# A two-layer transformer step on one NeuronCore: the terms of the last attention row are split two and two between GpSimd and VectorE, and every engine of the second layer gets another order

## The reference

```python
xn = _layernorm(x)
x = x + _L0_attn_ref(xn, ...) + _L0_ffn_ref(xn, ...)       # causal softmax attention, 16 heads of 64; gated FFN, 384 hidden
xn = _layernorm(x)
x = x + _L1_attn_ref(xn, ...) + _L1_ffn_ref(xn, ...)
```

```python
def step(W, qkvb_t):
    q_t, k_t, v_t, b_t = qkvb_t
    v_old = jnp.einsum('bhij,bhj->bhi', W, k_t)
    delta = b_t * (v_t - v_old)
    W_new = W + delta[..., :, None] * k_t[..., None, :]
    out_t = jnp.einsum('bhij,bhj->bhi', W_new, q_t)
    return (W_new, out_t)
```

## Time and profile before

| | before |
|---|---|
| median of 3 runs | 1667.04 us (1667.03 to 1667.09) |
| the profiled execution, its own time | 1666.79 us |
| its span, from the first to the last instruction | 1665.1 us |
| granted TensorE clock | 1.000 |
| busy: PE, weight load, DVE, ACT, POOL | 99%, 63%, 80%, 60%, 53% |
| instructions: PE, DVE, ACT, POOL | 9922, 2760, 2014, 685 |
| second layer, from VectorE's first step of it on | 1150.3 us to the end |

### The profile page before, as it was taken

One profiled execution on the slowest core, in us unless ns is written; L12 is line 12 of the kernel. 1 busy time (PEld: TensorE's weight loads), 2 busy tenths in 40 slices (PEclk: granted clock), 3 DMA queues, 4 the chain that ended last, 5 costly groups with the idle time before them and its releaser, 6 DMA issues.

```text
span 1665.1 us, 29161 instructions
## 1 busy us (share of the span) xinstructions
PE 1651.0 (99%) x9922; PEld 1043.5 (63%) x9922; DVE 1326.7 (80%) x2760; ACT 1002.1 (60%) x2014; POOL 885.7 (53%) x685
## 2 busy tenths in 40 slices
PE   9999999999999999999999999999999999999998
PEld 6566656665665566556655665555667767776767
DVE  5477777777777777777777777776999999999997
ACT  3256656665666566666666666666676666566562
POOL 2133333333433333433333433343999999999995
PEclk9999999999999999999999999999999999999999
DMA  8000000000000000000000000010000000000000
GB/s 181 26 1 1 1 1 1 2 1 1 1 1 1 1 1 1 1 1 1 2 1 1 1 1 1 2 26 1 1 1 7 7 1 7 1 7 7 1 7 14
DMA packets 30036, 13.55 MB, mean 8 GB/s; under 512 B 17066, under 2 KB 29380, under 8 KB 29892
## 3 DMA queue, kind: packets, MB, share of 16 engines
q1 hardware_dynamic: 29892, 11.70, 3.1%
HBM read 9.60 MB, written 2.10 MB: 7 GB/s over the span
## 4 chain that ended last, share of the span: by engine, by line
PE 95%; DVE 2%; issue 1%; ACT 1%; POOL 1%; SPq 0%; DMA 0%; DVEq 0%; ACTq 0%; POOLq 0%
PE pair L946 17%; PE flip L963 16%; PE accum L984 11%; PE pair L2692 9%; PE misc L911 7%; PE flip L2715 5%; PE misc L1030 4%; PE flip L2704 4%; PE misc L924 3%; PE accum L1008 3%; PE flip L2752 3%; PE accum L2704 2%; PE pair L874 2%; PE accum L2715 2%; PE accum L1012 2%; PE flip L2738 1%
## 5 line engine op out<-in xcount | busy, mean ns | idle before, releaser
L382 POOL TENSOR_SCALAR probs<-probs,recip 128x256 f32<-128x256 f32 (+5 forms) x448 | 331.3, 754 | 693.8 <-DVE recip L616 693.8
L457 ACT ACTIVATE probs<-pair,neg_max 128x768 f32<-128x768 f32 (+5 forms) x448 | 332.3, 750 | 209.2 <-DVE neg_max L598 209.2
L598 DVE TENSOR_REDUCE neg_max<-pair 128x1 f32<-128x768 f32 (+7 forms) x512 | 372.8, 754 | 32.6 <-PE pair L946 9.6
L963 PEld LDWEIGHTS flip<-ident,probs 128*128 128x128 f32 x2048 | 228.0, 141 | 142.3 <-issue 65.4
L946 PE MATMUL pair<-qk_sb 64*128 64x512 f32 (+3 forms) x1536 | 292.1, 505 | 1.8 <-ACT probs L457 1.0
L963 PE MATMUL flip<-ident,probs 128*128 128x128 f32 x2048 | 280.1, 277 | 1.8 <-ACT slots L419 1.8
L419 ACT ACTIVATE slots<-flip 128x512 f32<-128x512 f32 x320 | 183.8, 595 | 155.6 <-PE flip L963 155.6
L589 DVE TENSOR_TENSOR pair<-pair,mask 128x128 f32<-128x128 f32 x512 | 137.1, 292 | 80.2 <-PE pair L946 80.2
L984 PE MATMUL accum<-slots,v_sb 128*64 128x512 f32 (+3 forms) x1024 | 192.7, 519 | 0.0
L2692 PE MATMUL pair<-slow_sb,h_T 128*128 128x512 f32 x384 | 179.9, 594 | 1.2 <-ACT probs_last L457 1.0
L1524 POOL TENSOR_TENSOR prod<-xnT,qs 128x1024 f32<-128x1024 f32 (+3 forms) x32 | 180.2, 5639 | 0.9 <-DVE qs L2233 0.9
(11 more groups left out here) (216 smaller groups left out, 2538.7 us busy)
## 6 DMA issues: line engine op xcount, KB each, us to landing
out<-x SPq DMA_DIRECT2D x8, 256.0 KB, 2.3
x<-in_L_attn_x SPq DMA_DIRECT2D x3, 512.0 KB, 5.6
slow_sb<-in_L_attn_w_slow SPq DMA_DIRECT2D x3, 512.0 KB, 8.2
w_qk<-in_L_attn_qkv_w SPq DMA_DIRECT2D x2, 512.0 KB, 7.2
xn<-in_L_ffn_W SPq DMA_DIRECT2D x1, 1024.0 KB
x<-in_L_attn_x SPq DMA_DIRECT2D x2, 256.0 KB, 3.2
w_v<-in_L_attn_qkv_w SPq DMA_DIRECT2D x1, 512.0 KB, 7.5
bv_bc<-in_L_attn_qkv_b SPq DMA_DIRECT2D x1, 512.0 KB, 7.5
```

What stands on the lines that cost most here:

```text
L382: pool.tensor_scalar(part, part, recip[:, u % 2, row, h:h + 1], 0.0, ALU.mult, ALU.add).then_inc(scaled, 1)
L457: act.activation(dst, pair[h][:, lo:hi], ACT.Exp, bias=neg_max[:, u % 2, row, h:h + 1], accum_out=row_sum[:, u % 2, row, h:h + 1]).then_in ...
L598: dve.tensor_reduce(out=neg_max[:, u % 2, row, h:h + 1], in_=pair[h][:, lo:hi], axis=AX.X, op=ALU.max, negate=True).then_inc(max_ready, 1)
L963: last = pe.transpose(flips[bank][:, P * k:P * (k + 1)], src[:, P * k:P * (k + 1)], ident[:])
```

## The change

`HIGH` goes from 1 to 2: in tiles 0 to 6, GpSimd makes row 3's terms of keys 2 and 3 (before 1 to 3), and VectorE those of keys 0 and 1 (before 0). And every engine's list of calls in the second layer is another one, with `PLACES`, `given_at`, `exps_at`, `prods_at`, `sums_at` and two rows of `ADDED` to match. No function is changed. Two copies out of PSUM go from VectorE to ScalarE (`keep_small(0)` and `keep_row(7, 3, 1)`), and one copy of the first layer's last unit goes from ScalarE to VectorE.

```diff
-HIGH = 1
+HIGH = 2
...
 PLACES = {
-    (0, "project", 0, 1): 3, (0, "project", 0, 0): 3, (0, "nrm"): 0, (0, "hat"): 2, (0, "hidden", 1, 1): 1,
+    (0, "project", 0, 0): 4, (0, "project", 0, 1): 3, (0, "project", 1, 1): 4, (0, "nrm"): 2, (0, "hat"): 1,
...
@@ GpSimd
             key_products(5, 1)
+            query_products(5, 0)
+            residual(5)
             row3_high(4)
-            query_products(5, 0)
-            query_products(5, 1)
             sums(4, 3)
             key_products(5, 2)
+            query_products(5, 1)
...
@@ ScalarE
             act.wait_ge(ones_made, 1)
-            last_keep(UNITS - 1, 3, 0, 0, FLIP_BANK[3, 0, 0])
+            exps(0, 0, 0)
+            last_keep(UNITS - 1, 3, 0, 1, FLIP_BANK[3, 0, 1])
+            last_att(UNITS - 1, 1)
+            last_keep(UNITS - 1, 4, 1, 0, FLIP_BANK[4, 1, 0])
+            last_keep(UNITS - 1, 4, 0, 0, FLIP_BANK[4, 0, 0])
             exps(0, 0, 1)
```

More of the change, by code:

```diff
@@ new lines @@
+    (5, "hidden", 4, 1): 2, (5, "project", 2, 2): 4, (4, "row", 3, 0): 1, (4, "row", 3, 1): 0,
+    (5, "project", 3, 2): 3, (4, "join"): 1, (6, "hat"): 0, (5, "expert", 4): 2, (6, "project", 0, 0): 3,
+    (5, "hidden", 5, 0): 0, (6, "project", 0, 1): 4, (5, "row", 0, 0): 2, (5, "hidden", 7, 0): 2,
+    (5, "expert", 5): 0, (6, "project", 1, 1): 3, (5, "row", 0, 1): 2, (5, "hidden", 7, 1): 1,
+    (5, "hidden", 6, 1): 0, (6, "nrm"): 1, (5, "hidden", 6, 0): 2, (6, "project", 2, 1): 4, (6, "small"): 1,
@@ L1231 @@
+    (7, "project", 3, 2): 4, (7, "expert", 6): 1, (7, "score"): 0, (7, "row", 2, 1): 2, (7, "row", 2, 0): 0,
+    (7, "row", 1, 1): 2, (7, "expert", 7): 0, (7, "join"): 1, (7, "row", 3, 0): 2, (7, "row", 3, 1): 0,
 }
@@ L2424, in _ @@
             gather(2, 0)
+            sum_queries(2, 0)
+            keep(2, 2, 0)
             gather(2, 1)
-            row(1, 3)
-            sum_queries(2, 0)
             keep(2, 3, 1)
@@ L2537, in _ @@
             gather(5, 0)
+            sum_queries(5, 0)
             invert(5, 0)
+            keep(5, 3, 1)
+            mixing(5, 0)
             gather(5, 1)
[L2540 to L2541 removed]
+            keep(5, 2, 0)
             gather(5, 2)
[L2543 removed]
+            sum_keys(5, 1)
             invert(5, 1)
[L2545 removed]
+            gather(5, 3)
+            keep(5, 3, 0)
+            row(5, 0)
             sum_queries(5, 1)
[L2547 removed]
@@ L2561, in _ @@
-            mixing(5, 2)
+            keep(6, 0, 1)
             sum_keys(5, 3)
+            keep(6, 1, 1)
+            sum_queries(5, 3)
             gather(5, 6)
-            sum_queries(5, 3)
-            keep(6, 0, 0)
             gather(5, 7)
-            keep(6, 0, 1)
+            keep(6, 2, 1)
+            mixing(5, 3)
+            keep(6, 1, 0)
+            sum_queries(6, 0)
+            row(5, 3)
             logits(6)
-            mixing(5, 3)
+            inverse(6)
             gates(6)
-            keep(6, 1, 1)
@@ L2597, in _ @@
+            row(6, 1)
             mixing(6, 2)
-            row(6, 1)
-            sum_keys(6, 3)
-            gather(6, 7)
-            invert(6, 3)
+            keep(7, 0, 0)
             keep(7, 0, 1)
@@ L2864, in _ @@
+            join(0, 1)
+            expert(1, 4)
+            project(2, 0, 1)
+            flip_row(1, 0, 1)
+            hidden(1, 6, 1)
+            flip_row(1, 0, 0)
+            join(0, 2)
+            project(2, 0, 0)
+            hidden(1, 5, 1)
             join(0, 3)
@@ L3072, in _ @@
-            flip_scores(5)
-            flip_nrm(6)
-            expert(5, 7)
-            make_small(6)
+            join(4, 2)
+            project(6, 0, 1)
+            flip_row(5, 0, 0)
+            join(4, 3)
+            hidden(5, 7, 0)
+            expert(5, 5)
+            project(6, 1, 1)
+            flip_row(5, 0, 1)
+            hidden(5, 7, 1)
+            hidden(5, 6, 1)
+            flip_nrm(6)
+            hidden(5, 6, 0)
+            project(6, 2, 1)
+            make_small(6)
```

1769 lines of the change are left out of this document (859 added, 910 removed), and 34 rows, old and new, of tables (exps_at, prods_at, sums_at).

## The result

The changed kernel takes **1675.36 us** (median of 5 runs, 1675.15 to 1675.75); the kernel before took 1667.03 in runs beside them. The ratio is 1.005 with a 95% interval of 1.0039 to 1.0061: slower by 8.3 us, where 8.1 were forecast. The profiled execution has a span of 1673.6 us.

The account below looks back on a forecast made before the run. The prediction took VectorE as full, with TensorE close beside it. Terms of +7.5 - 0.3 + 0.9 = +8.1 us on the profiled 1666.79 gave 1674.9, as a median 1675.2 us, 0.5% slower; range 1672.5 to 1681.0.

Parts of the forecast that it names:

- VectorE is full in the kernel before: Second layer, 1150.2 to 1654.7 us: VectorE has only 0.8 us of its own time left, so added work comes out.
- Rivals 1 and 2: Not slower, GpSimd is the pace: about 1663, chance 0.05; no change, TensorE is the pace: 1666 to 1668, chance 0.06.
- Row 3 on VectorE: Multiply by the mixing numbers grows from 1024 to 2048 columns in 7 tiles, 1.07 us more each: +7.5 us.
- The other moves: TensorE, ScalarE and GpSimd have the same operations in another order: taken as 0, added waits bounded by some 6 us.
- Row 3 on GpSimd: 7 operations of 5.34 us shrink to an estimated 3.7, saving 11 us of GpSimd but worth 0 at the end.
- The seam: Between the layers, a projection ahead of the last join makes VectorE start the second layer later: +0.9 us, bounds 0 and 1.7.
- The tail: After row 3 of tile 7: 10.4 us, the same in both; up to 4.3 us if GpSimd's last product came late.
- Rival 3: The new order makes VectorE wait, at the tail or about a microsecond a tile: 1679 to 1683 us, chance 0.12.
- Rival 4, the port: VectorE's seven longer operations each wait for the GpSimd operation in progress: 17.5 us, so 1693, chance 0.01.

Follow-up runs that it names:

- b_dummy: Kernel before with one more 128x1024 reduction on VectorE, which nobody waits for, behind row 3 in tiles 0 to 6: 1674.22 us, ratio 1.0046.
- b_gp2: Kernel before with GpSimd multiplying only keys 2 and 3 in row 3, VectorE still key 0, key 1's term left out: 1666.76 us, ratio 0.9998.
- b_nob2: Kernel before with the output-bias product that opens each join left out on TensorE: 1666.03 us, ratio 0.9997.
- b_less: Kernel before with VectorE multiplying half of key 0's heads in row 3 and GpSimd the rest, order unchanged: 1673.18 us, ratio 1.0035.
- a_one: Changed kernel with VectorE multiplying key 0 alone in row 3, key 1's term left out, order and waits kept: 1674.90 us, ratio 1.0049.
- b_split: Kernel before with only the split of row 3 changed to two keys and two, every order as it was: 1681.44 us, ratio 1.0085.
- a_split1: Changed kernel with the split of before (GpSimd three keys, VectorE one) in the new order: 1696.97 us, ratio 1.0179.
- b_seam: Kernel before with only the projection of tile 0, s = 1, keys, moved ahead of the first layer's last join: 1668.40 us, ratio 1.0009.

## Why the prediction was right, and where it wasn't

**The total was right, and one of its steps failed.** By its own steps:

- *VectorE is full in the kernel before*: shown. An addition of 7.9 us came out with 7.5 (b_dummy), less GpSimd work with 0 (b_gp2), less TensorE work with under 1 (b_nob2). Rivals 1 and 2 fall with that. It is shown for work that is added. Work taken from VectorE was tried once (b_less), together with more for GpSimd, and nothing was gained.
- *Row 3 on VectorE, +7.5*: the size was right, 2279 ns against 1213. Its place as the cause was not: in the changed kernel the term can be taken out for 0.5 us (a_one). It lies beside waits for TensorE of nearly the same length.
- *The other moves, 0*: this is the step that failed. The prediction reasoned that both orders have the same operations, and put the order's cost at 0 beside a full VectorE. In the new order TensorE has 5.4 us more idle time, and the stretch stays over 511 us whatever of the work tried here is taken from either engine: with VectorE's extra load gone, the changed kernel is still 8.1 us slower than before, where this step had 0. The two costs are not added up; the larger counts, and they lie 0.5 us apart. The sum was right since it took one of two nearly equal things and left out the other. Nothing in the prediction says why they should be equal, so to that extent the hit was luck. And the split needs a new order: in that of before it cost 14.5 us.
- *Row 3 on GpSimd*: 3.63 us where 3.7 was estimated; worth 0, as said. Its idle time in the stretch rose from 28.8 to 511.71 - 463.89 = 47.8 us, by 19, inside the 15 to 20.
- *The seam, +0.9*: `set_up` at 1151.21, as forecast. As a price it misled. In the old order the move costs about 1.5, in the new one undoing it costs 1.5 at the full clock and 3.3 by the medians. The prediction said that VectorE has other work until the keys of s = 1 are there, in both orders. In the new order it has not: their `keep` steps come right behind, and without the move VectorE waits 1.75 us for them. That the move saves this was put at 0.
- *The tail*: 10.7 us, against 10.4, the last product in time by 0.44 us.
- *Rival 3*: VectorE waits 2.0 us in the stretch, 1.2 more than before, so it didn't happen as described. But what it named, an order that can't keep VectorE fed, is what the changed order would show with less work on VectorE (a_one).
- *Rival 4, the port*: it did not happen, and the reading behind it was wrong. The 15 operations of 2048 columns keep 2279 ns, with GpSimd at work in 463.9 of 511.7 us. But they have one input in SBUF, not two: their rows say `terms<-qk_sb,misc`, and the mixing numbers of VectorE lie in `misc`, a PSUM tile. The rule of the Trainium skill (SBUF — State Buffer, "Who interferes with whom") that was weighed there is about a VectorE instruction with two SBUF inputs. So the earlier trace rows say nothing for or against it, and no run here tests it.

What stays open: which places of the new order make the 8.1 us, how much of them is the price of making `row(t, 3)` free `vs[1]` in time, and how much a better order with the same split would save. No version tried was faster than the kernel before by more than its measurement can tell.

## What to carry to other kernels

When a forecast total comes true, take the term out again: a limit of the same length may lie beside it, and a view of one engine's busy time and waits can't show it. With two engines that hand PSUM places to one another, ask of each piece of work which handoff comes next and who is late there; a saving ahead of a point where the other engine is late is worth nothing. When a computation moves to another engine, list the buffers whose last reader changes, and look in that engine's queue for what stands ahead of the reader: here, in the order of before, that cost about as much again as the work itself.

## What the runs showed of the hardware

In two traces TensorE's granted clock fell after a long wait, and the wait so cost more than its length. Windows of b_split around its stall, with TensorE's busy time as the first value behind the length and the granted clock as the third from the end:

```profile
1284.00:1288.00 4.00, 3.51 (x21) 2.35 (x19) 3.76 (x10) 1.27 (x2) 4.00 (x2) 1.00 0.00 0
1288.00:1292.00 4.00, 0.00 (x0) 0.00 (x0) 3.87 (x10) 0.00 (x0) 1.48 (x1) 0.97 0.00 0
1292.00:1296.00 4.00, 2.17 (x3) 1.13 (x4) 1.78 (x2) 1.02 (x1) 3.20 (x2) 0.50 0.00 0
1296.00:1300.00 4.00, 4.00 (x15) 2.10 (x15) 0.12 (x1) 2.31 (x3) 3.92 (x3) 0.68 0.00 0
```

TensorE stood still for 6.33 us, then ran at 0.50 of full speed, which is the 1.2 GHz level; four records of 128x512 took 3.78 us instead of 1.88, so the stall cost it some 1.9 us more in that group alone. a_split1 shows the same with 3.52 us behind a wait of 5.06, at 0.66 in 1224 to 1228 us. More surprising is the profiled execution of b_seam: a wait of 1.14 us, a smaller gap ahead of the first hidden product and sixteen small products were followed by a granted clock of 0.52 and 0.63 in 1154 to 1158 us, and by the group of 3.38 us:

```profile
1152.00:1154.00 2.00, 2.00 (x18) 1.94 (x17) 1.93 (x8) 0.69 (x1) 0.00 (x0) 1.00 0.03 8
1154.00:1156.00 2.00, 2.00 (x4) 0.68 (x3) 1.53 (x9) 1.18 (x5) 0.00 (x0) 0.52 0.00 0
1156.00:1158.00 2.00, 2.00 (x4) 0.84 (x3) 1.86 (x7) 0.92 (x2) 0.00 (x0) 0.63 0.00 0
```

The busy column reads 2.00 of 2.00 in all three: a TensorE at half speed looks fully busy, and only the clock column tells. The ten other executions of the same program have a mean of 1.000 and took 0.7 to 1.2 us less, so the same program does not bring the fall each time. The kernel before shows it too: one of 21 executions took 1668.48 us at a mean of 0.999, the median being 1666.95. In the changed kernel itself the granted clock is 1.00 over the stretch; this has no part in its time.

Times by size: GpSimd's multiply by a broadcast number per head took 3.627 us for 2048 columns, 5.34 for 3072 and 6.20 for 3584, some 1.7 us for each 1024; VectorE's took 0.679 us for 512, 1.21 for 1024 and 2.28 for 2048.
